# A four-part routing, the normalisation of the next batches, and attention: another order in the opening of a two-layer kernel

## Chip, cores and metric

The kernel is one program on one core of a Trainium2 chip. The metric is the device time of one execution in microseconds. Its engines are TensorE (PE, with weight loads as PEld), VectorE (DVE), ScalarE (ACT), GpSimd (POOL) and SyncE (SP), which only issues transfers here. Each engine works through its own queue in the order in which the program was written; between engines there are semaphores.

## What is computed

Eight sequences of 512 tokens, width 256, all in float32. Layer 0 multiplies an attention by the SiLU of a mixture of 64 experts; layer 1 multiplies a selective scan (a state-space layer) by the SiLU of a forest of 8 binary trees. Cut to the lines that matter here:

```python
xn = _layernorm(x)
Q, K, V = X @ Wq, X @ Wk, X @ Wv                      # attention, 16 heads in 4 groups
attn = softmax(Q K^T * scale); A = attn V; s = X + A @ Wpost
logits = xn @ gate_w.T; scores = sigmoid(logits)      # routing, 64 experts in 8 groups of 8
sfc = scores + gate_bias
group_scores = top_k(sfc.reshape(n, 8, 8), 2)[0].sum(-1)
tmp = where(in the 4 best groups, sfc, -inf)
topk_idx = top_k(tmp, 8)[1]; topk_w = scores there, normalised * 2.5
pos = running count of tokens per expert, kept where pos < 256
x = x + s * silu(experts' outputs, weighted and added up)
...                                                    # layer 1
```

## The kernel before

**One order for all engines.** `in_order(E)` (line 152) is run once for each engine, each time with an object whose methods emit that engine's share of a step; a method that an engine doesn't have does nothing. So the order in which `in_order` calls the steps is the order of every engine's queue. Steps are Python generators that yield a cost in "units". `together(leader, (steps, share), ...)` (line 432) runs the leader, and after each of its yields lets each of the others run until it has used up share x cost units; what is owed starts at zero in each call, and a step that has been started is run to its end, so a call can overshoot by one step. `filling()` (line 217) is the one long filler: attention of batch 0, of batch 1, then trees and attention in turn. `fill(units)` and `fill_until(what, count)` draw from it later.

**The opening.** `first(b)` (line 443) is the layer norm, transposition and logits of batch b: `first_stats(b + 1)` (VectorE lines 1196 to 1208, a reciprocal root on GpSimd line 1602), `first_turn(b, c)` for two halves (VectorE normalises at line 1212, TensorE transposes at 1707, ScalarE copies at 937) and `first(b)` (TensorE logits line 1715, ScalarE sigmoid line 941, SyncE stores the normalised rows). It yields 2.0, 1.5, 1.5 and 1.5. `routing(part)` (line 176) is eight steps of 2.2 for two batches (8 tiles of 128 tokens); all but one matmul pair are on VectorE (`route`, line 1285). Its last instruction of step 4 makes the selection (line 1350), TensorE counts it in step 5 with two matmuls (line 1852), VectorE copies the counts (lines 1353, 1355) and goes on; in step 7 SyncE stores the weights. Part p needs the sigmoids of batches 2p and 2p + 1.

**Attention** (`attention(b)`, line 156) yields 2.0 for its begin, for each of four V products and two leading K and Q products, then for each of 69 steps, and 3.5 for each of four output products. A step n on TensorE does the scores of a pair (line 1785, at even n), the transposes of two steps ago (1790), and at odd n the values product (1802) and now and then a projection (1746) or the spreading of the row sums (1810). At odd n VectorE takes the row maxima of the pair (1259), and once in eight steps it multiplies by the inverse row sums (1272, at n % 8 == 4). ScalarE makes the exponentials (1056) and copies the transposes (1025).

**Behind it** come `table()` (34 steps, attention beside it at share 1.0), `experts()`, the gathers of the first combination, and the scan stage: 8 batches of 64 scan steps (VectorE lines 1543 and 1548, ScalarE 1168, GpSimd 1668 and 1674) with `fill(3.9 / 2)` around each half step, 2.4 per step once all attention is done. At the scan step with k == 22 of a batch (`HEAD_AT`) the code calls `fill_until("attention", b + 2)`: step 406 is that of batch 6.

The order at the top of `in_order`'s body, which the change replaces:

```python
    for b in range(2, NB):
        together(first(b), (filler, FILL_PER_FIRST))
        if b == 2:
            E.first_end()
        if b % 2:
            together(routing(b // 2 - 1), (filler, ATTENTION_PER_ROUTING))
    together(routing(PARTS - 1), (filler, ATTENTION_PER_ROUTING))
    together(table(), (filler, ATTENTION_PER_TABLE))
```

Of the kernel before, what the change touches and what calls it, by code (L numbers as in the profile page):

```python
# [7 lines left out]
NB, SEQ, DM = 8, 512, 256  # L8
# [28 lines left out]
PARTS = NT // ROUTE_TILES  # L37
# [12 lines left out]
LAG_SCAN, LAG_C, LAG_SUM = 1, 2, 3  # L50
ARENA = 22016

ATTENTION_PER_ROUTING, ATTENTION_PER_TABLE = 1.0, 1.0
FILL_IN_FIRST = 3.5
FILL_FIRST_ROWS, FILL_LAST_ROWS = 14.0, 6.0
FILL_PER_FIRST, FILL_PER_EXPERTS, FILL_PER_COMBINE, FILL_PER_HEAD = 1.0, 0.2, 1.6, 1.2
# [95 lines left out]
def in_order(E):  # L152
# [23 lines left out]
    def routing(part):  # L176
        for j in range(8):
            E.route(part, j)
            yield 2.2

    def table():
        for t in range(NT + LAG_SLOTS):
            E.table(t)
            yield 2.2
        E.table_end()
# [31 lines left out]
    def filling():  # L217

        for b in range(2):
            for half in range(2):  # L220
                E.att_ready(b, half)
        for b in range(NB + 2):
            if b < NB:
                yield from attention(b)
                done["attention"] = b + 1
            if b >= 1 and b - 1 < NB:
                while done["normed"] < b:
                    yield 0
                if b + 1 < NB:
                    E.att_load(b + 1)  # L230
                tree = trees(b - 1)
                yield next(tree)
                done["begun"] = b
                yield from tree
                done["trees"] = b

    filler, owed = filling(), [0.0]
# [190 lines left out]
    def run(g):  # L428
        for _ in g:
            pass  # L430

    def together(leader, *others):
        owed = [0.0] * len(others)
        for cost in leader:
            for j, (steps, share) in enumerate(others):
                owed[j] += share * cost
                while owed[j] > 0:
                    took = next(steps, None)
                    if took is None:
                        break  # L440
                    owed[j] -= took

    def first(b):
        if b + 1 < NB:
            E.first_stats(b + 1)
        yield 2.0
        for c in range(KC):
            E.first_turn(b, c)
            yield 1.5
        E.first(b)  # L450
        yield 1.5
# [4 lines left out]
    E.first_stats(0)  # L456
    for b in range(2):
        run(first(b))
    for b in range(2, NB):
        together(first(b), (filler, FILL_PER_FIRST))  # L460
        if b == 2:
            E.first_end()
        if b % 2:
            together(routing(b // 2 - 1), (filler, ATTENTION_PER_ROUTING))
    together(routing(PARTS - 1), (filler, ATTENTION_PER_ROUTING))
    together(table(), (filler, ATTENTION_PER_TABLE))
    E.a_const()
    E.ssm_weights()
# [34 lines left out]
def build_program(nc, X, Wq, Wk, Wv, Wpost, gateT, gate_bias, w_gate, w_up, w_down, ln_gb, WinT, WxT, WdtT,  # L503
# [265 lines left out]
    def _(sp):  # L769
# [5 lines left out]
        class Sync(Parts):  # L775
# [134 lines left out]
            def end(self):  # L910
# [5 lines left out]
                w.wait_ge(wg_out, 16 * TWO * EXPERTS // PER_GROUP)  # L916

        in_order(Sync())

    @block.scalar  # L920
    def _(act):
# [7 lines left out]
        class Scalar(Parts):  # L929
# [255 lines left out]
            def end(self):  # L1185
                for i in range(2):
                    w.wait_ge(y_out[i], 16 * EXPERTS // 2)

        in_order(Scalar())

    @block.vector
    def _(dve):
# [38 lines left out]
        class Vector(Parts):  # L1231
# [346 lines left out]
            def ssm_fin(self, b, i):  # L1578
# [11 lines left out]
                dve.tensor_tensor(x1[:, sl, i, :], o, x1[:, sl, i, :], ALU.add).then_inc(ssm_fin, 1)  # L1590

        in_order(Vector())

    @block.gpsimd
# [483 lines left out]
```

## Time and profile before

| | |
|---|---|
| median of 3 runs | 2654.51 us (2651.61 to 2655.56) |
| the profiled execution | 2673.1 us, its span 2671.0 us |
| mean granted TensorE clock | 0.94 |
| opening, up to the first table instruction on VectorE | 233.7 us |
| table, up to the experts' first gathers | about 84 us |
| experts and first combination | about 318 to 690 us |
| scan stage | about 780 to 2640 us |

The times of stages are read from the starts of their instructions in the trace. The profile gives, for a stretch of time, how long each engine was busy, and for an instruction that its engine stood still before it, what released it ("<-"). A wait stands on the engine that waited; an instruction behind it in the same queue is late by as much. Stretches named in the prediction are us from the span's start.

### The profile page before, as it was taken

Reading aid. Unit: us, or ns where it says so; the run is one execution under the profiler, and the core shown is the slowest. Engines: PE = TensorE matmul, PEld = TensorE weight load, DVE = VectorE, ACT = ScalarE, POOL = GpSimd, SP = SyncE. Lnnn points to the kernel's source line nnn. Section 1 sums busy time; section 2 is a strip of 40 time slices with the busy share of each in tenths; the row PEclk is TensorE's granted clock in tenths of the full one; section 3 lists DMA queues with packets and bytes.
Section 4 is the critical chain, followed back from the end, with each engine's and each line's share of the span. In section 5 each row is a group of like instructions: output and inputs, shape, how many; then the busy total and the mean of one; then the engine's idle time right before and its main releaser. Section 6 shows DMA issues by size and latency. Waiting matters only on the chain.

```text
span 2671.0 us, 37912 instructions
## 1 busy us (share of the span) xinstructions
PE 2218.0 (83%) x13128; PEld 1411.8 (53%) x13128; DVE 1862.8 (70%) x2832; ACT 1762.4 (66%) x3266; POOL 1738.8 (65%) x1416
## 2 busy tenths in 40 slices
PE   6677879999688879898989898889889988888761
PEld 4444557776445546555655465456445644564441
DVE  5878544543246877687668767876778667789888
ACT  3556633446367876888588867796778677766862
POOL 1000254424767988788888789887977797656566
PEclk9888989999899999999989999999999999999895
DMA  4000258874566668654765486448534754477776
GB/s 157 25 21 5 84 157 230 236 214 91 93 121 131 123 118 184 135 113 97 182 128 112 86 200 121 97 95 187 118 86 91 179 122 90 93 166 162 181 171 152
DMA packets 280191, 344.22 MB, mean 129 GB/s; under 512 B 64063, under 2 KB 209664, under 8 KB 280000
## 3 DMA queue, kind: packets, MB, share of 16 engines
q0 software_dynamic: 84080, 175.67, 35.1%
q1 hardware_dynamic: 175248, 144.83, 19.0%
q10 hardware_dynamic: 20672, 21.30, 2.3%
q8 instruction: 104, 1.70, 0.3%
q14 instruction: 87, 0.71, 0.1%
HBM read 198.00 MB, written 26.80 MB: 84 GB/s over the span
## 4 chain that ended last, share of the span: by engine, by line
POOL 24%; PE 16%; issue 14%; ACT 9%; DVE 9%; DMA 2%; POOLq 0%; DVEq 0%; SPq 0%; ACTq 0%
POOL arena L1668 9%; POOL acc_sb L1646 6%; POOL arena L1674 4%; POOL arena L1684 4%; DVE bank L1543 3%; PE bank L1785 2%; PE bank L1790 2%; PE bank L1802 2%; PE bank L1840 2%; ACT PT L1025 2%; PE bank L1917 2%; PE bank L1948 1%; ACT Pr L1056 1%; ACT bank L1168 1%; PE bank L1746 1%
## 5 line engine op out<-in xcount | busy, mean ns | idle before, releaser
L1668 POOL TENSOR_TENSOR arena<-arena 128x512 f32<-128x512 f32 x512 | 877.3, 1791 | 18.2 <-DVE arena L1534 16.1
L1646 POOL DMA_INDIRECT acc_sb<-ybuf,slot_idx x256 | 423.1, 1653 | 128.3 <-DMA ybuf<-arena 64.3
L1259 DVE TENSOR_REDUCE negmax<-bank 128x1 f32<-128x512 f32 x512 | 328.2, 682 | 200.6 <-PE bank L1785 199.9
L1168 ACT ACTIVATE bank<-arena,A_sb 128x512 f32<-128x512 f32 x512 | 354.4, 697 | 163.3 <-DVE arena L1548 136.4
L1543 DVE TENSOR_TENSOR_SCAN bank<-bank,arena 128x512 f32<-128x512 f32 x320 | 389.9, 1218 | 82.9 <-ACT bank L1168 45.3
L1674 POOL TENSOR_TENSOR arena<-arena 128x512 f32<-128x512 f32 x192 | 298.7, 1556 | 207.8 <-DVE arena L1543 207.7
L1025 ACT COPY PT<-bank 128x512 f32<-128x512 f32 x512 | 298.1, 592 | 200.9 <-PE bank L1790 171.5
L1056 ACT ACTIVATE Pr<-bank,negmax 128x512 f32<-128x512 f32 x512 | 353.3, 701 | 103.1 <-DVE negmax L1259 102.8
L1790 PEld LDWEIGHTS bank<-ident,Pr 128*128 128x128 f32 x2048 | 234.6, 147 | 288.8 <-ACT Pr L1056 225.1
L1785 PE MATMUL bank<-Kp,Qp 64*128 64x512 f32 x1024 | 307.6, 666 | 87.2 <-ACT PT L1025 52.1
L1790 PE MATMUL bank<-ident,Pr 128*128 128x128 f32 x2048 | 312.0, 292 | 59.4 <-ACT Pr L1056 58.6
L1684 POOL DMA_DIRECT2D arena<-arena x255 | 285.8, 1121 | 112.1 <-DVE arena L1548 111.9
L1802 PE MATMUL bank<-PT,V_sb 128*64 128x128 f32 x4096 | 288.0, 284 | 2.6 <-DVE AT L1272 2.6
L1802 PEld LDWEIGHTS bank<-PT,V_sb 128*64 128x64 f32 x4096 | 224.9, 139 | 86.2 <-issue 82.4
L1543 DVE TENSOR_TENSOR_SCAN arena<-bank,arena 128x512 f32<-128x512 f32 x192 | 232.2, 1209 | 39.1 <-ACT bank L1168 27.1
L1548 DVE TENSOR_TENSOR arena<-bank,arena 128x512 f32<-128x512 f32 x320 | 221.1, 691 | 11.0
L1637 POOL DMA_INDIRECT arena<-rows,arena x128 | 129.1, 1009 | 122.6 <-DVE arena L1451 55.5
L1785 PEld LDWEIGHTS bank<-Kp,Qp 64*128 64x128 f32 x1024 | 84.8, 192 | 158.4 <-ACT PT L1025 75.8
L1746 PE MATMUL bank<-xaT,Wq_sb 128*128 128x512 f32 x256 | 132.3, 641 | 15.6 <-ACT PT L1025 10.0
L1840 PE MATMUL bank<-Wpost_sb,AT 128*128 128x256 f32 x512 | 121.7, 398 | 24.0 <-DVE AT L1272 19.6
L1893 PE MATMUL bank<-arena 128*128 128x256 f32 x512 | 128.6, 395 | 13.5 <-DVE arena L1473 8.8
L1840 PEld LDWEIGHTS bank<-Wpost_sb,AT 128*128 128x128 f32 x512 | 101.4, 200 | 42.7 <-DVE AT L1272 21.3
(216 smaller groups left out, 3676.7 us busy)
## 6 DMA issues: line engine op xcount, KB each, us to landing
arena<-arena POOLq DMA_DIRECT2D x255, 512.0 KB, 5.3
arena<-bc_dram SPq DMA_DIRECT2D x256, 256.0 KB, 3.9
ybuf<-arena ACTq DMA_DIRECT2D x64, 256.0 KB
arena<-in_w_gate SPq DMA_DIRECT2D x64, 128.0 KB
arena<-in_w_up SPq DMA_DIRECT2D x64, 128.0 KB
arena<-in_w_down SPq DMA_DIRECT2D x64, 128.0 KB
arena<-in_X SPq DMA_DIRECT2D x8, 512.0 KB, 6.8
s_sb<-in_X SPq DMA_DIRECT2D x8, 512.0 KB
```

The source lines that it names most:

```text
L1025: act.copy(PT[:, m % RING_P, :, :].rearrange("p a b -> p (a b)"), bank[m % RING_S_ATT][:, :]).then_inc(att_pt, 1)
L1056: act.activation(Pr[:, m % RING_P, :], bank[m % RING_S_ATT][:, :], ACT.Exp, bias=negmax[:, m % RING_STAT:m % RING_STAT + 1], accum_out=row ...
L1168: act.activation(bank[DECAY[g % 2]][:, :], dt_sb[:, size_slot(b, cb), :], ACT.Exp, scale=A_sb[:, cb, n:n + 1]).then_inc(ssm_decay, 1)
L1259: dve.tensor_reduce(negmax[:, m % RING_STAT:m % RING_STAT + 1], bank[m % RING_S_ATT][:, :], AX.X, ALU.max, negate=True).then_inc(att_max, 1)
L1543: dve.tensor_tensor_scan(v if c_by_pool(m) else decay, decay, v, 0.0, ALU.mult, ALU.add).then_inc(ssm_scan, 1)
L1646: pool.indirect_dma_start(acc_sb[:, i, :], None, ybuf, bass.IndirectOffsetOnAxis(ap=slot_idx[:, b * TILES + i, k:k + 1], axis=0), bounds_c ...
L1668: pool.tensor_tensor(st_sb[:, g % RING_S, :], u_sb[:, size_slot(b, cb), :], B_sb[:, load % RING_BC, :], ALU.mult).then_inc(ssm_input, 1)
L1674: pool.tensor_tensor(v, v, C_sb[:, load % RING_BC, :], ALU.mult).then_inc(ssm_c_pool, 1)
L1684: pool.dma_start(whole(xy[:, b % 2, cb - PAIR_CB + 1:cb + 1, :]), whole(st_sb[:, first:first + PAIR_CB, :]), accum_op=ALU.add).then_inc(ss ...
L1785: pe.matmul(bank[m % RING_S_ATT][:, :], Qp[own, p % 2, i * P:(i + 1) * P], Kp[own, twin(p) % 2, :], start=True, stop=True).then_inc(att_sc ...
L1790: ins = pe.transpose(bank[m % RING_S_ATT][:, c * P:(c + 1) * P], Pr[:, m % RING_P, c * P:(c + 1) * P], ident[:, :])
L1802: ins = pe.matmul(bank[AV][j * HD:(j + 1) * HD, i * P:(i + 1) * P], V_sb[:, c, g * HD:(g + 1) * HD], PT[:, (m + j) % RING_P, c, :], start= ...
```

## The change

The loop over batches and routings is replaced. The first of batch 2 stands alone as before. Then each routing part is a leader with two kinds of steps beside it: the firsts of batches 3 and 4 beside part 0, 5 and 6 beside part 1, 7 beside part 2, none beside part 3, at 0.8 units for one of the routing; and attention's steps at 1.4 for one (1.0 before). What is left of the firsts after a part runs with attention at 1.0.

```diff
-ATTENTION_PER_ROUTING, ATTENTION_PER_TABLE = 1.0, 1.0
+ATTENTION_PER_ROUTING, ATTENTION_PER_TABLE, FIRSTS_PER_ROUTING = 1.4, 1.0, 0.8
...
-    for b in range(2, NB):
-        together(first(b), (filler, FILL_PER_FIRST))
-        if b == 2:
-            E.first_end()
-        if b % 2:
-            together(routing(b // 2 - 1), (filler, ATTENTION_PER_ROUTING))
-    together(routing(PARTS - 1), (filler, ATTENTION_PER_ROUTING))
+    together(first(2), (filler, FILL_PER_FIRST))
+    E.first_end()
+    for part, beside_it in enumerate(((3, 4), (5, 6), (7,), ())):
+        firsts = itertools.chain.from_iterable(map(first, beside_it))
+        together(routing(part), (firsts, FIRSTS_PER_ROUTING), (filler, ATTENTION_PER_ROUTING))
+        together(firsts, (filler, FILL_PER_FIRST))
```

## Rows read from the trace of the kernel before

**Rows 1.** The page, part 1: busy us, share of the span, instructions, per engine.

```profile
PE 2218.0 (83%) x13128; PEld 1411.8 (53%) x13128; DVE 1862.8 (70%) x2832; ACT 1762.4 (66%) x3266; POOL 1738.8 (65%) x1416
```

**Rows 2.** Busy time by stretch of the opening : columns PE, PEld, DVE, ACT, POOL, clock, DMA share, GB/s.

```profile
81.40:104.50 23.10, 18.89 (x137) 13.59 (x137) 13.56 (x42) 16.12 (x34) 3.04 (x4) 0.85 0.13 46
104.50:139.70 35.20, 20.53 (x156) 12.00 (x154) 32.69 (x88) 15.99 (x34) 0.00 (x0) 0.87 0.04 8
139.70:160.10 20.40, 19.51 (x134) 12.64 (x135) 10.36 (x29) 14.91 (x31) 1.21 (x2) 0.90 0.15 53
...
199.20:233.70 34.50, 21.10 (x126) 12.07 (x127) 33.17 (x88) 12.94 (x31) 0.00 (x0) 0.75 0.04 8
51.40:233.70 182.30, 126.96 (x844) 78.50 (x845) 151.91 (x407) 90.57 (x193) 4.25 (x6) 0.84 0.06 18
```

**Rows 3.** Waits of VectorE from 51.4 to 233.7 us: total us, times, longest us.

```profile
DVE negmax L1259 <- PE bank L1785: 17.7, 9, 6.0
DVE AT L1272 <- PE bank L1802: 6.2, 4, 3.0
DVE arena L1353 <- PE bank L1852: 1.2, 2, 0.7
```

**Rows 4.** The page, part 5: groups of instructions (busy, mean ns, idle before and releaser).

```profile
L1259 DVE TENSOR_REDUCE negmax<-bank 128x1 f32<-128x512 f32 x512 | 328.2, 682 | 200.6 <-PE bank L1785 199.9
...
L1056 ACT ACTIVATE Pr<-bank,negmax 128x512 f32<-128x512 f32 x512 | 353.3, 701 | 103.1 <-DVE negmax L1259 102.8
...
L1785 PE MATMUL bank<-Kp,Qp 64*128 64x512 f32 x1024 | 307.6, 666 | 87.2 <-ACT PT L1025 52.1
L1790 PE MATMUL bank<-ident,Pr 128*128 128x128 f32 x2048 | 312.0, 292 | 59.4 <-ACT Pr L1056 58.6
...
L1802 PE MATMUL bank<-PT,V_sb 128*64 128x128 f32 x4096 | 288.0, 284 | 2.6 <-DVE AT L1272 2.6
...
L1746 PE MATMUL bank<-xaT,Wq_sb 128*128 128x512 f32 x256 | 132.3, 641 | 15.6 <-ACT PT L1025 10.0
```

**Rows 5.** Timeline from 86 to 92 us, all engines: start us, us, engine, line, operation.

```profile
86.14 1.11 PE L1707 MATMUL bank<-ident,arena 128*128 128x128 f32 x4 [2.02 <-DVE arena L1212]
...
87.29 0.59 ACT L937 COPY xn<-bank 128x512 f32<-128x512 f32 x1 [2.55 <-PE bank L1707]
...
90.13 0.66 PE L1707 MATMUL bank<-ident,arena 128*128 128x128 f32 x4
...
90.25 0.69 DVE L1272 TENSOR_TENSOR AT<-bank,inv_bc 128x512 f32<-128x512 f32 x1 [2.97 <-PE bank L1802]
...
90.71 1.13 PE L1785 MATMUL bank<-Kp,Qp 64*128 64x512 f32 x4
```

**Rows 6.** Timeline of VectorE from 50 to 58 us.

```profile
50.22 1.29 DVE L1259 TENSOR_REDUCE negmax<-bank 128x1 f32<-128x512 f32 x2 [16.24 <-PE bank L1785]
51.42 0.68 DVE L1316 SCALAR_TENSOR_TENSOR arena<-arena 128x512 f32<-128x512 f32 x1
...
53.75 1.28 DVE L1259 TENSOR_REDUCE negmax<-bank 128x1 f32<-128x512 f32 x2
54.95 0.68 DVE L1328 TENSOR_TENSOR arena<-WinT_sb 128x512 f32<-128x512 f32 x1
...
57.84 0.69 DVE L1336 TENSOR_REDUCE WinT_sb<-arena 128x64 f32<-128x512 f32 x1
```

**Rows 7.** Timeline of TensorE from 47 to 50 us.

```profile
47.23 1.89 PE L1715 MATMUL bank<-arena,acc_sb 128*128 128x64 f32 x16
49.06 1.99 PE L1785 MATMUL bank<-Kp,Qp 64*128 64x512 f32 x8
```

**Rows 8.** Busy time of one batch's part of the scan stage, columns as in rows 2.

```profile
1055.00:1300.00 245.00, 217.54 (x1284) 133.71 (x1283) 182.56 (x242) 190.32 (x364) 201.58 (x159) 0.97 0.61 129
```

**Rows 9.** VectorE's scan instructions (line 1543) late in the span: us, busy (count), clock, DMA.

```profile
2490.00:2591.00 101.00, 43.38 (x36) 0.95 0.75 171
2591.00:2634.00 43.00, 27.05 (x23) 0.54 0.89 196
```

## The prediction, made before the changed kernel ran

> **What bounds the kernel now.** I read the busy times of the whole span first, then the busy times stage by stage, then what VectorE waits for in the opening, and last the instructions around the longest wait. Over the span TensorE is busy 83% and no engine is full [rows 1], so a mean says little. The change acts on the opening, before the table, which ends at about 233.7 us. From 51.4 us on it alternates between two kinds of stretch [rows 2]. In the routing stretches (of which 104.5 to 139.7 and 199.2 to 233.7 are shown) VectorE is busy 93 and 96% and TensorE 58 and 61%. In the two stretches of normalisation and logits (81.4 to 104.5, 139.7 to 160.1) it is the other way: VectorE 59% and 51%, TensorE 82% and 96%. Over the whole 182.3 us VectorE works 151.9 us and stands still 30.4 us. Waits of any length make 25.1 us of that [rows 3]: 17.7 for attention's scores before the row maximum, 6.2 for the values product, 1.2 for routing's own counting matmul. The other 5.3 us are gaps of some hundredths between dependent instructions, and they stay. The four routings are one chain on VectorE whatever stands beside them; so VectorE's work plus its waits is the length of this stage.
>
> **What moves.** One call of `first` is worth 6.5 units, one routing 8 x 2.2 = 17.6, an attention step 2. Before, attention gets 6 x 6.5 + 4 x 17.6 = 109.4 units and a round-up in each of ten calls of `together`, and stands at step 52 of batch 0 when the table begins. After, it gets 6.5 + 4 x 24.64 = 105.1 units with five round-ups and stands at step 48: **four attention steps fewer in the opening**. The firsts beside a routing get 0.8 x 17.6 = 14.1 units and need 13, so they finish inside it and the last call of the loop finds nothing. No instruction is added or removed; the sigmoid and exponential groups keep their number and alternation.
>
> **VectorE's sum.** (a) Four attention steps less: 4 x 0.64 of row maximum [rows 4] and one product with the row sums of 0.69 [rows 5], 3.3 us. (b) At 34.0 us VectorE has only the maximum left in front of it and stands still 16.2 us for the first scores [rows 6]. After, the next batch's statistics and normalisation, and two routing steps, stand there instead. The routing steps are 2.3 us (51.42 to 53.75) and 2.9 us (54.95 to 57.84), together 5.2 us. The scores themselves don't come sooner: TensorE works without a gap up to 49.06 [rows 7], the logits that stood ahead of them (1.89 us) move behind, but they had covered ScalarE's copy of Q. So the first maximum still ends at 51.4 us, with 5.2 us more done before it. Work left after it: 151.9 - 3.3 - 5.2 = 143.4, with the gaps 148.7 us.
>
> (c) The waits. With two or more pieces of VectorE work between two pairs of maxima, a pair's scores are there in time: the round trip from one pair's maxima to the scores of the pair after the next is about 6.3 us (maxima 1.3, exponentials 1.4, transposes 1.2, the last copy 0.6, scores 1.2, values 0.6) [rows 4, 5], and between them now lie 2.6 routing steps of some 3.6 us. So the waits in the two normalisation stretches go (most of the 17.7), and the products of values are covered by the routing step ahead of them. New waits come where a normalisation feeds TensorE and VectorE next needs a result that is queued on TensorE behind it. Each time it is transposes 1.1, copy 0.6, transposes 0.7, scores 1.1 [rows 5], 3.5 us together. This stands open once in full in the second part (batch 5's transposes sit just ahead of scores 12 and 13). In the first two parts the sixth routing step waits for counting matmuls that are queued behind a batch's first transposes and an attention step: 3.3 and 2.1 us. The two others cost 1.0 together, as now. Three pairs in the last two parts with only 1.6 to 2.8 us of routing between them cost 1.5 us each. Sum 3.5 + 5.4 + 1.0 + 4.5 = 14.4; some will lie behind one another, so I take **13 us**. The bounds are 3 and 25.1, what is waited now; nearer to half of today's, since most of today's are in stretches that no longer exist.
>
> The table then begins at 51.4 + 148.7 + 13 = 213.1 instead of 233.7 us: **20.6 us sooner**, between 8.5 (waits of 25.1) and 30.6 (waits of 3).
>
> SyncE's and the GpSimd's queues are moved past as well. The row stores follow the same normalisations and nobody waits for them before the table, the store of the weights waits for the routing's sixth step as before, and the short reciprocal roots on GpSimd follow their statistics with a routing step of 1.6 us or more before the normalisation that needs them.
>
> **What comes back later.** The four steps are done at some time. Table, experts and combination each keep their number of attention pieces, shifted by four, so their length stays. In the scan stage attention is paced by units per scan step and stays four steps late until step 406, where the code makes it finish batch 7 at once; these four steps are caught up there, and the debt of 8 units puts the end of the last tree four scan steps later (485 for 481). Price from above: TensorE's 0.60 + 0.61 + 0.56 + 0.26 = 2.03 us per step (scores, transposes, values and a share of the projections, each group's busy time over 512 steps) [rows 4], over its share of 0.89 in the scan stage [rows 8]: 4 x 2.28 = 9.1 us. From below: four scan steps that run at the pace beside trees, 101/36 = 2.81 us, instead of VectorE's own, 43/23 = 1.87 us [rows 9]: 3.8 us. I take 7, nearer the upper end, since the catch-up stands still in front of scan steps.
>
> Net: 20.6 - 7 = 13.6 us. The profiled execution took 2673.1 us (span 2671.0), 0.7% above the median of the runs, 2654.5. A difference of this size is the same on both, so the **forecast is 2640.9 us**.
>
> **Where the skill says otherwise.** Stretches with opposite busy engines are what is laid together here [rows 2]. The Trainium skill, Perfetto Trace Analysis, section Optimization Strategy, says that kernels whose most-contended engine changes over time may gain from interleaving those regimes; by that rule, taken whole, the fuller engine would set the length and all 25.1 us of waits would go (the first rival). The granted clock from 51.4 us on is a mix of its two levels (1.2 and 2.4 GHz), on average 0.84; in the last routing, where TensorE is busy 21.1 of 34.5 us, it is 0.75, and 0.90 where it is busy 19.5 of 20.4 us. The Trainium skill, TensorE: Matmul & The Clock Gate, section What's actually happening, says that throttled is the resting state and activity releases it; by that, 1.4 attention units per routing unit would lift the clock in the routings, which helps the waits of (c) and nothing else, and speaks for the same rival.
>
> **The rivals.**
> - *All of the waits go* or the late steps cost nothing. For the former, 148.7 us instead of 182.3 is 33.6 sooner, less 7: 2627.9 us. For it: the round trip has cover nearly everywhere. Against: the 3.5 us above, and the routing's own wait for its counts can't go entirely.
> - *The waits only change places.* TensorE's queue now holds attention, the turns of a new batch and the counts in one order, and each waits for VectorE or ScalarE with the others behind it; if that gives 25 us again, 8.5 - 7 = 1.5 us are left: 2653.0 us. For it: TensorE is 70% busy at a clock of 0.84, and 12 attention steps per part at the low clock level cost twice their time. Against: VectorE stood still 9.5 and 10.0 us in the two stretches that are gone.
> - *Slower: the catch-up at scan step 406.* TensorE and VectorE take four more attention steps there in a row while scan steps wait behind them, and the normalisation of batch 7 follows from it. If that costs over 3 us for each step, the chain of batch 7's inputs is late by more than 12 us. With 14 us, and the opening giving only 8.5, this is 2660 us. It decides from the point where the late steps cost more than the opening gives. Against: TensorE's own work for the four is 8.1 us, and VectorE's 2.6 us has place beside it.
> - *It doesn't do what it says* can be left out of the sum: the order above follows from the costs in the code.
>
> **How the numbers follow.** Forecast 0.55 (2632 to 2650), all waits gone 0.19, waits change places 0.18, slower 0.08. A comparison of runs tells about 0.2%, 5.3 us, from no change. The forecast's case and the first rival are nearly all beyond it; a part of the forecast's lower gains is not, so faster 0.75, same 0.17, slower 0.08. The range goes from 2621 to 2656: below it reaches the opening's full 33.6 us with late steps that cost nothing (2620.9), above past the second rival, and it leaves out the third.
>
> **What would show it.** Right: the table's first instruction on VectorE between 203 and 225 us, VectorE's share from 51.4 us to it at 0.87 to 0.95, its wait for the first scores cut from 16.2 to about 7 us, waits of 2 to 4 us ahead of the sixth routing step of the first two parts. The table lasts 84 us and the experts as long as now. The end of the last tree comes nearer to the span's end. Wrong: more than 25 us of waits left in the opening; a scan stage longer by over 10 us; or a table that grows because TensorE brings a backlog into it.

## The result

The changed kernel is slower. Its median is 2682.55 us over six runs (2678.27 to 2693.38), that of the kernel before beside it 2655.38 (2651.61 to 2669.58): a ratio of 1.0097 with a 95% interval of 1.0078 to 1.0115, 27 us more. The forecast was 2640.9 us, so sign, size and range (2621 to 2656) were wrong. The profiled execution took 2679.99 us, its span 2677.9 us. The lines of its kernel are one lower than before's (L1258 for L1259).

The page, parts 1 and 5, against [rows 1] and [rows 4]:

```profile
PE 2219.0 (83%) x13090; PEld 1413.3 (53%) x13128; DVE 1855.7 (69%) x2832; ACT 1766.5 (66%) x3269; POOL 1739.0 (65%) x1416
...
L1258 DVE TENSOR_REDUCE negmax<-bank 128x1 f32<-128x512 f32 x512 | 328.2, 682 | 192.3 <-PE bank L1784 191.3
...
L1784 PE MATMUL bank<-Kp,Qp 64*128 64x512 f32 x1024 | 309.5, 671 | 83.1 <-ACT PT L1024 36.6
```

The work is the same, on every engine within 0.4%. What differs lies between instructions, so only a view by stages finds it. Busy time of five stretches, cut at the first maximum's end, the table's first instruction, its end, the first scan step and the last instruction; columns as in [rows 2]:

```profile
0.00:51.40 51.40, 28.85 (x128) 22.36 (x128) 24.33 (x85) 15.53 (x27) 8.68 (x18) 1.00 0.61 204
51.40:222.10 170.70, 122.57 (x787) 76.75 (x790) 143.69 (x391) 85.48 (x178) 4.18 (x6) 0.84 0.07 19
222.10:304.80 82.70, 72.21 (x1426) 49.06 (x1427) 59.66 (x102) 66.73 (x112) 3.31 (x1) 1.00 0.04 12
304.80:741.50 436.70, 376.17 (x2098) 271.60 (x2097) 189.43 (x391) 192.57 (x434) 234.14 (x199) 0.96 0.70 176
741.50:2674.80 1933.30, 1619.23 (x8658) 993.54 (x8690) 1438.18 (x1866) 1406.19 (x2520) 1488.66 (x1193) 0.95 0.60 131
```

The table begins 11.6 us sooner (233.7 before), and the scan stage, 1895.2 us before, is 38.1 us longer. Two questions follow: why the opening gave 11.6 and not 20.6 us, and where four late attention steps, priced at 7 us, find some 40.

VectorE's waits in the opening, as in [rows 3], and the three rows of its timeline that hold most of them or answer to [rows 6]:

```profile
DVE negmax L1258 <- PE bank L1784: 11.8, 6, 4.4
DVE arena L1352 <- remote: 8.1, 3, 4.7
DVE AT L1271 <- PE bank L1801: 1.8, 2, 1.4
```
```profile
50.21 1.29 DVE L1258 TENSOR_REDUCE negmax<-bank 128x1 f32<-128x512 f32 x2 [8.11 <-PE bank L1784]
...
65.65 0.69 DVE L1352 COPY arena<-bank 128x512 f32<-128x512 f32 x1 [4.69 <-remote]
...
102.16 1.29 DVE L1258 TENSOR_REDUCE negmax<-bank 128x1 f32<-128x512 f32 x2 [4.40 <-PE bank L1784]
```

The wait for the first scores fell from 16.2 to 8.1 us, the maximum ends where it did, and VectorE's work from there to the table is 143.7 us where 143.4 was forecast. The waits are 21.9 us (with 0.2 for an issue), not 13. The wait for the counts (L1352; "remote" is a release that the profile ties to no instruction) grew from 1.2 to 8.1 us.

### The profile page after: what moved, and what is told of

It is laid out like the page before. It is cut to its first block, busy times and chain, and to the rows that moved or that the text cites. A ratio compares the mean times of both kernels' runs of the same rounds, so it can differ in the third digit from the quotient of the medians.

```text
span 2677.9 us, 37877 instructions
## 1 busy us (share of the span) xinstructions
PE 2219.0 (83%) x13090; PEld 1413.3 (53%) x13128; DVE 1855.7 (69%) x2832; ACT 1766.5 (66%) x3269; POOL 1739.0 (65%) x1416
## 4 chain that ended last, share of the span: by engine, by line
POOL 22%; PE 18%; issue 14%; ACT 11%; DVE 7%; DMA 1%; another core or an unknown queue 0%; POOLq 0%; DVEq 0%; ACTq 0%
POOL arena L1667 9%; POOL acc_sb L1645 6%; POOL arena L1673 4%; POOL arena L1683 3%; DVE bank L1542 3%; PE bank L1784 2%; PE bank L1839 2%; PE bank L1801 2%; PE bank L1789 2%; ACT PT L1024 2%; PE bank L1947 2%; ACT Pr L1055 2%; PE bank L1745 2%; ACT bank L1167 2%; PE bank L1916 2%
## 5 line engine op out<-in xcount | busy, mean ns | idle before, releaser
L1667 POOL TENSOR_TENSOR arena<-arena 128x512 f32<-128x512 f32 x512 | 875.2, 1789 | 14.6 <-DVE arena L1533 14.1
L1258 DVE TENSOR_REDUCE negmax<-bank 128x1 f32<-128x512 f32 x512 | 328.2, 682 | 192.3 <-PE bank L1784 191.3
L1892 PE MATMUL bank<-arena 128*128 128x256 f32 x512 | 125.8, 389 | 13.7 <-DVE arena L1472 13.7
```

Of the source, the lines that this page charges most:

```text
L1258: dve.tensor_reduce(negmax[:, m % RING_STAT:m % RING_STAT + 1], bank[m % RING_S_ATT][:, :], AX.X, ALU.max, negate=True).then_inc(att_max, 1)
L1667: pool.tensor_tensor(st_sb[:, g % RING_S, :], u_sb[:, size_slot(b, cb), :], B_sb[:, load % RING_BC, :], ALU.mult).then_inc(ssm_input, 1)
```

## The experiments

Each ratio is against runs of the kernel before on the same chip. Stage lengths are from each kernel's one profile. The two numbers in the edits are the units of filler drawn before the experts (`FILL_FIRST_ROWS`) and after the first combination (`FILL_LAST_ROWS`); a unit is half an attention step.

**How far one profile can be trusted.** The kernel before and the changed one, profiled again.

> The kernel before once more, for a second profile: the first one took 2673.1 us where the median of the runs is 2655.4, and its experts' stage (first gather to first gather of the combination) took 313.6 us against 296.4 after the change, with the same work. If that is a disturbance of one execution, this profile has the experts at about 297 us and a span near 2655; if the old order makes the experts slower, it has 313 us again.

> The changed kernel once more, beside the other three on one chip, as the reference of this call: 1.010 of before, a scan stage near 1933 us, and the first expert's transposes about 10 us behind the end of the table (19 us in before) if that gap belongs to the order and not to one execution.

The kernel before took 2665.91 us beside 2669.16 there, span 2663.8 us. The changed one came out at 1.0111 (1.0062 to 1.0160), span 2700.9 us. The scan stages nearly repeat: 1895.2 and 1894.8 us before, 1933.3 and 1940.0 after. Over all eight profiles, of this and the later runs, that have before's order in that stage it lasts 1894.8 to 1900.7 us, and up to 4.6 us of that spread lie in its first batch. What doesn't repeat is the way from the table's end to the first scan step: 455.3 and 448.4 us before, 436.7 and 452.7 after. So the first profile of the changed kernel has that stage short and the first of before has it long, and the spans are only 7 us apart (2677.9 and 2671.0) where the medians are 27 apart. From here on the second profile of each is the one compared, unless the text says otherwise.

**The late steps alone.** The kernel before with its old opening, but eight units fewer in front of the experts: from there on the order is the changed kernel's.

```diff
-FILL_FIRST_ROWS, FILL_LAST_ROWS = 14.0, 6.0
+FILL_FIRST_ROWS, FILL_LAST_ROWS = 6.0, 6.0
```

> The opening of before; behind the table attention gets 8 units (four steps) less, so that from the experts on the order of all queues is that of the changed kernel. Theory A (the scan stage pays for the phase in which attention, trees and the scan's own side work now stand to each other): the loss of the scan stage is all here, 30 to 40 us slower than before, about 2690 us. Theory B (four attention steps cost what they weigh on TensorE, and the rest of the loss comes from something the new opening leaves behind): 2660 to 2665 us. Theory C (the stage is full of TensorE work and what the opening saves can't be kept): within 2655 to 2660 us.

1.0135 (1.0110 to 1.0160), 36 us slower, with a scan stage of 1936.3 us. Being four steps late makes the whole loss, without anything of the new opening.

**The opening alone.** The changed kernel with the eight units given back before the experts.

```diff
-FILL_FIRST_ROWS, FILL_LAST_ROWS = 14.0, 6.0
+FILL_FIRST_ROWS, FILL_LAST_ROWS = 22.0, 6.0
```

> The new opening; behind the table attention gets 8 units (four steps) more, so that from the experts on the order of all queues is that of before. Theory A: the opening's gain of about 12 us less the 8 us of the four steps behind the table is kept whole, 2645 to 2652 us. Theory B: slower than before by the loss less 8 us, 2670 to 2675. Theory C: about as before, 2655 us.

0.9990 (0.9980 to 1.0000). The scan stage is back at 1894.9 us, and the table still begins at 222.1 us. But the first transposes for the experts start 30.1 us after the table's end (20.0 and 19.2 in before's two profiles), and the first scan step 461.6 us after it instead of 448.4: the four steps take there what the opening had saved.

**Giving back later, and owing more, less or nothing.** The changed kernel, and then the kernel before, with other amounts in the second place or in both:

```diff
 k4: changed -FILL_LAST_ROWS 6.0   +14.0
 k6: before  -FILL_LAST_ROWS 6.0   +14.0
 k11: before -FILL_LAST_ROWS 6.0   +2.0
 k5: before  -14.0, 6.0            +4.0, 0.0
```

> The changed kernel, with the four attention steps that its opening leaves out handed back behind the first combination (8 more units there) instead of ahead of the experts. From the end of the first combination on the order of all queues is that of before; the experts run with the attention steps that they have in the changed kernel. In the trace of the changed kernel the scan stage began at 741.5 us against 765.9 in a second profile of before. Theory A (position of the filler): the scan stage has its old 1894.8 us again and the start keeps 24.4 us less 8 for the four steps, so 0.99 to 0.995 of before. Theory C (what the opening saves is lost anyway, the stage is full): 1.00. If the early start was only the place of the steps around the experts' first transfers, some of it stays here too, since the experts' surroundings are those of the changed kernel.

> Before, with 8 units more behind the first combination, so that attention is four steps ahead through the scan stage. Amount theory: as fast as before or faster, 0.99 to 1.00. Alignment theory: four steps are half a cycle in this direction too, so slower by about as much as four late without the catch-up, 1.008 to 1.012.

> Before, with 4 units less behind the first combination: attention is two steps late through the scan stage. Known so far: four ahead 0.9955, none 1, four late 1.0135, eight late 1.010. Amount theory: 1.003 to 1.007, with a catch-up at scan step 406 of half the length. Packing theory (each position has its own sum of small waits, without an order): anything between 0.995 and 1.015.

> Before, with attention eight steps late from the scan stage on (10 units less ahead of the experts, 6 less behind the first combination). Four steps late cost 1.35% (36 us). Amount theory (every step that attention is late costs, since the inputs of the next batch and the end of attention come nearer to their due times): eight steps late cost more than four, 1.02 of before or more. Alignment theory (attention has a cycle of eight steps with a projection and a spreading at fixed places, and four is half a cycle, eight a whole one): the scan stage is nearly as before except for a longer catch-up at scan step 406, 1.00 to 1.01.

| run | attention at the scan stage | ratio | scan stage, us |
|---|---|---|---|
| k6 | 4 steps ahead of before | 0.9955 (0.9934 to 0.9976) | 1887.2 |
| k1 | as before | (one run) | 1894.8 |
| k4, new opening | as before | 0.9957 (0.9933 to 0.9981) | 1900.5 |
| k11 | 2 late | 1.0013 (0.9999 to 1.0028) | 1904.0 |
| k2 | 4 late | 1.0135 (1.0110 to 1.0160) | 1936.3 |
| k5 | 8 late | 1.0101 (1.0052 to 1.0151) | 1934.0 |

Two steps cost 9 us of scan stage against k1 (3 to 9 against the eight profiles with before's order), four cost 41, eight no more than four. A price for each step can't give that. Nor can a pattern of eight steps, by which eight late would be as none late but for the catch-up: k5's batches up to batch 5 take 1519.7 us instead of 1501.7, so 18 of its 39 us lie ahead of the catch-up. What is left is which pieces fall on which scan steps. In k4 the changed kernel keeps a gain: 0.43%, about 11 us. No run tells here how much of it would come with the old opening, from moving the four steps behind the first combination alone.

**The catch-up at scan step 406.** The changed kernel, with an eighth of a unit more in each scan step of batch 5, so that attention is where it was before from step 384 on:

```diff
-  ... FILL_PER_STEP if b else FILL_IN_FIRST) - work
+  ... FILL_PER_STEP if b else FILL_IN_FIRST) - work + (0.125 if b == 5 else 0)
```

> The changed kernel, with 8 units more of filling spread over the 64 scan steps of batch 5, so that from scan step 384 on attention and trees stand where they stand in before. With the four steps caught up in a row at scan step 406 the part from 384 to the end took 225.5 + 183.8 = 409.3 us against 393.1 in before. Theory A1 (the row is what costs there, on top of the four steps' own 8 us): 384 to the end is back to 393 us, batch 5 grows by at most 8 us (266 for 258), the total is 0.997 of the changed kernel or less, 1.005 to 1.008 of before. Theory A2 (the steps cost the same wherever they are done): batch 5 grows by 15 us and the total stays at 1.011.

1.0046 (1.0028 to 1.0064), against 1.0097 and 1.0111 for the changed kernel in two other sessions: some 14 to 17 us of its loss, uncertain by 7 us or more, since the ratios come from different sessions. The last two batches take 389.1 us instead of 409.3 in the changed kernel's second profile, and batch 5, which now does the four steps, takes 1 us more. TensorE around the catch-up in the kernel before, the changed one (its first profile here; the second has the same waits of 4.00 and 12.70 us) and k8:

```profile
2354.46 14.08 PE L1840 MATMUL bank<-Wpost_sb,AT 128*128 128x256 f32 x64 [0.79 <-DVE AT L1272]
...
2376.70 1.03 PE L1924 MATMUL bank<-PT,path_sb 128*128 128x512 bf16 x2 [2.86 <-DVE PT L1497]
```
```profile
2362.09 15.77 PE L1839 MATMUL bank<-Wpost_sb,AT 128*128 128x256 f32 x64 [4.00 <-DVE AT L1271]
...
2395.86 0.63 PE L1923 MATMUL bank<-PT,path_sb 128*128 128x512 bf16 x1 [12.70 <-DVE PT L1496]
```
```profile
2371.55 14.08 PE L1839 MATMUL bank<-Wpost_sb,AT 128*128 128x256 f32 x64 [0.91 <-DVE AT L1271]
...
2393.79 0.60 PE L1923 MATMUL bank<-PT,path_sb 128*128 128x512 bf16 x2 [2.86 <-DVE PT L1496]
```

The last things of a batch's attention are four output products of 16 matmuls, 3.5 us each; the 64 matmuls stand in one row on TensorE in all three. VectorE adds each to the sum, and has scan steps between those additions or not. The scans around the widest gap, before and changed (first profile):

```profile
2358.56 1.22 DVE L1543 TENSOR_TENSOR_SCAN bank<-bank,arena 128x512 f32<-128x512 f32 x1
...
2362.01 1.22 DVE L1543 TENSOR_TENSOR_SCAN bank<-bank,arena 128x512 f32<-128x512 f32 x1
...
2369.70 1.23 DVE L1543 TENSOR_TENSOR_SCAN bank<-bank,arena 128x512 f32<-128x512 f32 x1
```
```profile
2361.95 1.22 DVE L1542 TENSOR_TENSOR_SCAN bank<-bank,arena 128x512 f32<-128x512 f32 x1
...
2379.02 1.22 DVE L1542 TENSOR_TENSOR_SCAN bank<-bank,arena 128x512 f32<-128x512 f32 x1
```

Before, two of the four products stand between scan steps, and the widest gap from one scan's start to the next is 7.7 us. In the changed kernel all four stand in the catch-up, and that gap is 17.1 us (17.0 in the second profile). The scan steps that were held up then run in front of the tree's decision on VectorE (L1496), and TensorE stands still 12.7 us for it instead of 2.9. In k8 both are back to 7.7 and 2.9. The last two batches hold 14.1 us more of TensorE's work in the changed kernel (286.9 us for 272.8) and are 16.1 us longer: nothing there takes it in. By count the changed kernel has four attention steps more there (8 matmuls of scores, 16 transposes, 48 of values), with their projections 9.9 us of busy time; most of the rest is matmuls of equal number that last longer (line 1948: 64.7 us for 59.5). In k8 that work is in the batches up to 5 (1352.8 us for 1339.3), and they are 0.7 us longer for it (1531.4 for 1530.7).

**Where the rest lies.** Busy time of scan batches 0, 3, 6 and 7 of the kernel before (its second profile), then of the changed kernel (its first):

```profile
765.90:999.00 233.10, 199.53 (x1206) 119.87 (x1207) 173.20 (x223) 190.84 (x364) 192.60 (x155) 0.97 0.62 127
...
1505.30:1753.40 248.10, 223.79 (x1270) 138.94 (x1266) 185.13 (x242) 190.62 (x352) 211.04 (x167) 0.99 0.59 129
2267.50:2480.70 213.20, 175.92 (x869) 107.56 (x870) 181.62 (x239) 154.13 (x259) 130.02 (x112) 0.94 0.65 149
2480.70:2660.70 180.00, 96.84 (x304) 59.91 (x302) 153.13 (x187) 94.70 (x127) 110.04 (x98) 0.78 0.73 163
```
```profile
741.50:979.40 237.90, 202.46 (x1188) 120.69 (x1190) 172.35 (x223) 193.57 (x364) 192.90 (x156) 0.96 0.62 125
...
1489.80:1749.40 259.60, 226.42 (x1257) 139.81 (x1261) 187.94 (x243) 190.69 (x352) 211.04 (x167) 0.97 0.56 123
2265.00:2490.80 225.80, 186.10 (x940) 113.95 (x944) 185.09 (x246) 156.26 (x269) 130.04 (x112) 0.93 0.61 138
2490.80:2674.80 184.00, 101.24 (x299) 62.72 (x304) 152.36 (x185) 96.66 (x131) 109.99 (x98) 0.77 0.73 162
```

Batch 3 is 11.5 us longer with only 2.6 us more work on TensorE; its idle time is 33.2 us instead of 24.3. The eight batches differ by 4.8, 2.5, 1.7, 11.5, 2.7, -1.2, 12.5 and 4.1 us. The 4.8 of batch 0 is little more than what one order shows there from profile to profile (233.1 to 237.7 us). The second profile of the changed kernel has 29.1 us more up to batch 5, with 3.5 us more work on TensorE: there the loss is standing still, not work. k2 and k8 have batch 3 at 259.5 and 260.5 us, with a different opening and a different later part, so its loss comes from the four steps' place alone. Eight late have it at 260.4, two late at 253.1. By the starts of the scan steps on GpSimd (line 1668), at which the batches are cut too, it lies in three places: scan steps 192 to 200, 208 to 216 and 248 to 256 are 4.6, 2.8 and 3.5 us longer, in the changed kernel's first profile and in k2 alike. Which pair of instructions makes it wait there I haven't settled.

**The weights that stream in before the experts.** As the table ends, SyncE and ScalarE issue the experts' first weights and the second layer's together. The stretch from the table's end to the first transposes for the experts in the changed kernel's two profiles, and TensorE's row in the second:

```profile
304.80:315.30 10.50, 10.50 (x87) 6.36 (x86) 4.27 (x10) 7.38 (x19) 7.35 (x7) 1.00 1.09 355
```
```profile
305.10:321.60 16.50, 11.46 (x83) 6.49 (x82) 4.25 (x10) 7.38 (x18) 11.87 (x12) 0.88 0.86 279
```
```profile
318.70 2.08 PE L1784 MATMUL bank<-Kp,Qp 64*128 64x512 f32 x4 [4.92 <-issue]
```

One program, the same instructions, 10.2 us (the first window is 0.3 us wider) and 16.5 us: in the second TensorE waits 4.9 us for nothing that the profile shows, and ScalarE 5.0. To see whether this sets the time, the kernel before was run with the second layer's weights issued behind the experts:

```diff
-    E.ssm_weights()
     E.exp_begin()
     fill(FILL_FIRST_ROWS)
     together(experts(), (filler, FILL_PER_EXPERTS))
+    E.ssm_weights()
```

> Before, with the four loads of the scan stage's weights (1.8 MB on ScalarE's queue) issued behind the experts instead of ahead of them. Seven attention steps between the end of the table and the first expert's transposes took 19.2 and 20.0 us in two profiles of before, and 10.2 and 16.5 in two of the changed kernel, with engines standing still for 5 to 9 us without a partner that was late. Theory D (instructions' own loads queue behind this burst of 3.8 MB): with half of the burst gone the stretch is 14 us or less in every profile and the kernel is 0.997 of before. Rival (the stalls are attention's own waits): as before, 19 us, 1.000.

The stretch became 13.7 us, with no "remote" wait left in it (ScalarE's longest was 5.6 and 4.7 us in before's two profiles). But of eight profiles with before's order and its loads up to there, at 14.4 to 20.0 us, the shortest (k11) has such waits of 0.8 us only. So one profile at 13.7 doesn't show that the stalls hang on that stream of transfers; it stays a guess. And table's end to first scan step is 449.7 us (448.4 in before's second profile), and the ratio 1.0006 (0.9985 to 1.0027): whatever is won in front is given back in the experts' part.

**Interleaving without the missing steps.** The changed kernel with 1.5 for 1.4 units beside the routing. That puts the four attention steps back into the opening, and from the table on the order is exactly before's.

```diff
-ATTENTION_PER_ROUTING, ... = 1.4, 1.0, 0.8
+ATTENTION_PER_ROUTING, ... = 1.5, 1.0, 0.8
```

> The changed kernel with attention at 1.5 units for one of the routing instead of 1.4: attention stands at step 52 when the table begins, and from the table on the order of all queues is that of before, instruction for instruction. So this is the new opening by itself. The table began 11.6 to 15 us sooner with four steps less; the four steps cost VectorE 3.3 and TensorE 8.1 us. Theory A (the loss of the changed kernel is all in the position of the filler): the table begins 6 to 10 us sooner, all of it is kept, 0.995 to 0.998 of before. Theory C (what the opening saves is lost later): 1.000. Theory E (something else in the new opening costs later): above 1.002.

1.0005 (0.9991 to 1.0020). The table begins at 234.3 us, as before. VectorE's opening in it, and its waits:

```profile
51.40:234.30 182.90, 122.39 (x852) 76.33 (x851) 146.87 (x397) 91.88 (x195) 3.64 (x6) 0.83 0.06 18
```
```profile
DVE negmax L1258 <- PE bank L1784: 17.4, 6, 4.0
DVE arena L1352 <- PE bank L1851: 7.0, 3, 3.8
DVE AT L1271 <- PE bank L1801: 6.7, 3, 3.1
```
```profile
85.77 1.97 PE L1789 MATMUL bank<-ident,Pr 128*128 128x128 f32 x8 [9.86 <-ACT Pr L1055]
```

So the rearrangement alone gives nothing: the 5.0 us of work that no longer lie behind the first maximum (146.9 us for 151.9) are eaten by waits of 31.1 us instead of 25.1. The last row (TensorE's) shows the other side of it. From 69.39 to 84.22 VectorE goes through two routing steps of 7.2 and 7.6 us with no maximum before the second has ended, and TensorE has nothing for 9.9 us. It stands like that four times in this opening, for 8.5 to 12.0 us (three times for exponentials, once for ScalarE's copy of Q). Beside the short steps TensorE gets as much attention as beside the long ones, and VectorE waits for it. All eight steps are charged 2.2 units and are 0.6 to 7.7 us long.

**An even grain.** k10 with the routing cut into ten steps instead of eight, each charged by its length; then the kernel before with the same cut and no interleaving.

```diff
-        for j in range(8):
+        for j, cost in enumerate((1.8, 1.5, 1.8, 1.0, 2.1, 2.6, 1.8, 3.0, 1.7, 0.4)):
             E.route(part, j)
-            yield 2.2
+            yield cost
```

> k10_share_15 with the two long routing steps cut in two and with costs in proportion to their VectorE time (1.8, 1.5, 1.8, 1.0, 2.1, 2.6, 1.8, 3.0, 1.7, 0.4, together 17.7); from the table on the order is that of before. Uneven steps as the cause: TensorE's waits of 12 us beside the long steps and half of VectorE's 31 us of waits go, the table begins at 218 to 225 us instead of 234.3, and the kernel is 0.994 to 0.997 of before. Rival (attention's round trip through three engines sets the pace, whatever the grain): the table begins within 3 us of 234 and the kernel is 1.000.

> Before, with the same cut and the same costs of the routing steps, firsts and routings one after the other as before. Uneven steps as the cause: in the old order VectorE waited only about 6 of its 25 us in the routing stretches, so little is to be had, a table at 229 to 233 us. If it gains as much as k12_new_even, the even grain is worth something by itself and the interleaving nothing.

k12 is at 0.9909 (0.9882 to 0.9935), 24 us faster than before; its table begins at 209.9 us, 24.4 us before k10's. From the table on it has before's order, and the profile keeps nearly all of the gain: first scan step 23.6 us sooner than in before's second profile, end 22.4 us sooner. k14 is at 0.9990 (0.9976 to 1.0005), its table at 229.4 us. VectorE's opening in k12, its waits, and then k14's:

```profile
51.40:209.90 158.50, 120.32 (x833) 74.31 (x833) 142.22 (x372) 90.62 (x191) 3.62 (x6) 0.88 0.07 21
```
```profile
DVE negmax L1258 <- PE bank L1786: 9.4, 4, 3.2
DVE arena L1352 <- PE bank L1853: 1.4, 2, 1.1
DVE AT L1271 <- PE bank L1803: 0.6, 1, 0.6
```
```profile
51.40:229.40 178.00, 129.82 (x850) 81.01 (x851) 151.61 (x406) 91.04 (x193) 4.24 (x6) 0.87 0.06 19
```
```profile
DVE negmax L1259 <- PE bank L1787: 17.0, 7, 6.0
DVE AT L1272 <- PE bank L1804: 3.0, 1, 3.0
```

VectorE's waits are 11.4 us in k12, 19.7 less than in k10, and 4.7 us less of its work lies behind 51.4: together the 24.4. TensorE's waits for exponentials and for the normalisation, in k10 and in k12, show most of the cause gone:

```profile
PE bank L1789 <- ACT Pr L1055: 35.4, 5, 12.0
PE bank L1706 <- DVE arena L1211: 11.0, 3, 5.0
```
```profile
PE bank L1708 <- DVE arena L1211: 19.5, 4, 8.6
PE bank L1791 <- ACT Pr L1055: 13.9, 8, 5.2
```

The long waits beside the long steps are 21.5 us shorter; 8.5 us come back ahead of the normalisation's transposes. Neither half does it alone: interleaving by itself 1.0005, the even grain by itself 0.9990, both together 0.9909. Cutting the two long steps and charging each step by its length were changed together; which of the two matters more no run tells.

**Both findings.** k12 with eight units more in the second place, as in k4 and k6 (`FILL_LAST_ROWS` 14).

> k12_new_even with 8 units more behind the first combination, as in k6_four_ahead, which was 0.9955 of before. If the two gains add up: 0.990 to 0.993 of before. If the start that the opening gains is lost in the first batch of the scan stage, as 5 us of it were in k4_new_late_fill, 0.994.

2634.43 us beside 2668.68, 0.9871 (0.9846 to 0.9897). It beats both kernels: by 1.3% the one before, and by about 2.3% the changed one, from the two ratios. The scan stage is 1886.5 us, the table begins at 209.8 us.

## Why the prediction was wrong, step by step

*Four steps fewer:* right. With eight units taken from the kernel before (k2) or given to the changed one (k3), the scan stage of each is the other's.

*(a) and (b), VectorE's work:* right in size, 143.7 us for 143.4, the first maximum at its old place, the table's length 82.7 us for 84. But (a)'s worth was mis-sized. I put the four steps in as their 3.3 us of work on VectorE. Between the changed kernel and k10 they are 3.2 us of work and 9.2 us of waits. VectorE's share from 51.4 us on came out at 0.84, below the 0.87 that I had named as a sign of being right. It isn't the interleaving that brought the table forward in this change, but the steps it left out.

*(c) 13 us of waits:* wrong, 21.9 us; 31.1 us with the four steps back. The failed step is "between them now lie 2.6 routing steps of some 3.6 us". That is a mean. The steps are 0.6 to 7.7 us long at the same price, so beside a long one TensorE runs dry and beside a short one VectorE waits. k12 charges each step by its length, and there the waits are 11.4 us: the argument on the round trip holds only under that condition, which I didn't name. For the opening the second rival was right: waits that change places, 22 to 31 us for its 25. I had forecast waits of 3.3 and 2.1 us at the first two counts; the first was 4.7, the second 1.2 and a third 2.2.

*Table, experts and combination keep their length:* right within a few us. Table's end to first scan step is 448.4 us in k1 and in k10; with the changed order it is 449.7 in k2 and 452.7 in the changed kernel's second profile. The profiles of one program differ there by up to 16 us, however, and with it "a difference of this size is the same on both" had no ground: before's profiled execution was 18.6 us above its median, some 7 of them in this stage (455.3 for 448.4 in the second profile), and the changed kernel's was 2.6 us below its own.

*The price of the late steps, 7 us:* wrong by a factor of six, and the reason for the sign. Scan stages of the changed order are 38 to 45 us longer, k2's 41. The step that failed is costing four mean steps by TensorE's share, 2.03 us each [rows 4]. Three things were missed.
- The work of the four steps was nearly right, 9.9 us where my sum had 8.1. What it left out is the place: they are caught up at the end of a batch's attention, so that all four output products stand in a row on VectorE where scans stood between two of them. The last two batches hold 14.1 us more of TensorE's work and are 16.1 us longer, and k8 puts 14 to 17 us of the run's time on the place.
- A pace by units moves every piece, not the last four only. Up to batch 5 each piece has other neighbours than before, and that is 21.9 us in the changed kernel's first profile and 29.1 in its second, some 12 of them in batch 3. My "stays four steps late until step 406" took the stage up to there as unchanged and put no price on it.
- The bounds of 3.8 and 9.1 us were both made from work. The part up to batch 5 is standing still, and busy times give no bound for it. Which instructions wait for which there stays open; what is shown is that the steps' place alone brings it (k2, k3).

*The third rival* named the mechanism at its place: more than 3 us for each late step in the catch-up, 14 us in all. k8 puts 14 to 17 us on it. Its chance of 0.08 was too low, and its time of 2660 us too fast, since it held the rest of the scan stage unchanged.

*Why I weighed it so:* each of the terms above asks how much work moves. With four engines and in-order queues, the trace says what stands still, and that is a property of the neighbours. What I could have read beforehand is which pieces stand before step 406 (64 matmuls of 14.08 us in one run of TensorE, with VectorE's scans between them), and that the routing's steps at one price were 0.6 to 7.7 us long.

*The skill's rule.* In this kernel, interleaving the stretches of opposite busy engines gives 1.0005 as it is and 0.9909 with even steps; the first rival's 33.6 us are not reached even then (the table begins 23.8 us sooner than before). The Trainium skill, Perfetto Trace Analysis, section Optimization Strategy, which says that regimes with different contended engines may gain from being interleaved, fits the trace only once the grain is even. The granted clock of the opening is 0.84 in the changed kernel as before, 0.83 in k10 and 0.88 in k12, where TensorE is busy 76% of the stretch instead of 67%. By the Trainium skill, TensorE: Matmul & The Clock Gate, section What's actually happening, activity is what releases the clock; the rows agree in direction. I put no price on it, since k14 has 0.87 as well and gains 4 us.

## What to carry to other kernels

Before work is interleaved between two engines, list the lengths of the leader's steps and charge each by its own: equal prices for unequal steps only move the waits. When a change alters how much filler is drawn early, hold the later order fixed, or price it by what stands at each forced catch-up and in the batches between, and measure that alone: here drawing eight units (four steps) later cost 36 us with no other edit. And compare a stage over several profiles before a difference of 10 us between two profiles is given a cause.

## What the runs showed that was not expected

- The time is not monotonic in how late the filler is: 2 steps 1.0013, 4 steps 1.0135, 8 steps 1.0101, and 4 ahead 0.9955.
- At the start of the experts, with the DMA engines' share near 1 and 355 GB/s moved, engines stand still up to 5 us (9.2 us on VectorE in k3) with nothing that the profile can name; the stretch varies between 10.2 and 16.5 us in one program, and between 14.4 and 20.0 over eight profiles with before's order; why, no run shows.
- Two profiles of the changed program differ by 23 us of span, 16 of it between the table's end and the scan stage.
